# Two transposes of a transformer block moved from TensorE and ScalarE to transposing transfers, and VectorE's small tiles moved to PSUM

## The reference

```
# branch 1: linear attention, 16 heads of 16
qkv = x @ Wqkv.T + bqkv ;  q, k, v = split(qkv)
q = elu(q * scale) + 1 ;   k = elu(k * scale) + 1
y = q * cumsum(k * v) / clip(sum_d(q * cumsum(k)), 1e-3)
x = layernorm(x + y @ Wproj.T + bproj)
# branch 2: feed-forward in block floating point, blocks of 32 share a power of two
h = gelu(quant(x) @ quant(w_fc).T + b_fc)            # 256 -> 1024
x = layernorm(x + quant(h) @ quant(w_proj).T + b_proj)   # 1024 -> 256
```

## Time and profile before

| | |
|---|---|
| runs of the kernel before | 281.45, 281.32, 280.38 us; median 281.32 us |
| the profiled execution | 282.59 us |
| its span (first to last instruction) | 280.8 us |
| PE busy | 252.6 us, 90% |
| DVE busy | 243.3 us, 87% |
| ACT busy | 168.8 us, 60% |
| POOL busy | 169.9 us, 60% |
| mean granted TensorE clock | 0.976 of full speed |

### The profile page before, as it was taken

The page is one execution under the profiler, slowest core; times in us unless marked ns, Lnnn a source line. Parts: engine busy times, 40 slices in busy tenths (PEclk is TensorE's granted clock), DMA queues, the critical chain, the costliest instruction groups (busy, mean ns, idle before and its releaser), DMA issues.

```text
span 280.8 us, 4189 instructions
## 1 busy us (share of the span) xinstructions
PE 252.6 (90%) x1476; PEld 158.1 (56%) x1476; DVE 243.3 (87%) x505; ACT 168.8 (60%) x278; POOL 169.9 (60%) x113
## 2 busy tenths in 40 slices
PE   5798998999999999999999999999999998858650
PEld 4545553665575656675676557655766565633330
DVE  2289788989899989999899989998999999987941
ACT  0563426757669576848676856866694766345712
POOL 1056365666856594777568666759565947763831
PEclk9799799999999999999999999999999999999995
DMA  6930020002001300030002200220001000200202
GB/s 162 363 76 2 0 75 2 0 2 75 0 2 49 103 1 1 2 120 30 2 0 75 78 1 0 77 75 0 2 25 50 4 0 0 77 1 0 75 2 75
DMA packets 13556, 11.82 MB, mean 42 GB/s; under 512 B 3040, under 2 KB 13280, under 8 KB 13536
## 3 DMA queue, kind: packets, MB, share of 16 engines
q1 hardware_dynamic: 11904, 11.28, 12.5%
q10 hardware_dynamic: 1632, 0.27, 0.6%
HBM read 7.35 MB, written 4.19 MB: 41 GB/s over the span
## 4 chain that ended last, share of the span: by engine, by line
DVE 51%; PE 34%; POOL 4%; ACT 3%; issue 3%; DMA 3%; ACTq 1%; POOLq 0%; DVEq 0%
PE abank L964 19%; DVE h_amax L748 11%; DVE stats L722 7%; DVE kvsum L700 6%; DVE hq L659 5%; PE dbank L1028 4%; DVE y L712 3%; DVE r L716 3%; DMA Wproj_sb<-in_L_attn_Wproj_dram 3%; DVE h_pow L651 2%; PE tbank L1021 2%; PE bbank L996 2%; DVE kv L690 2%; DVE r L760 2%; PE hbank L1014 2%
## 5 line engine op out<-in xcount | busy, mean ns | idle before, releaser
L964 PE MATMUL abank<-xT,WqkvT 128*128 128x512 f32 x176 | 85.3, 609 | 0.8 <-ACT xT L429 0.8
L323 POOL TENSOR_TENSOR h_round<-h,h_inv 128x1024 f16<-128x1024 f32 x32 | 73.7, 2302 | 16.2 <-DVE h_inv L654 16.2
L964 PEld LDWEIGHTS abank<-xT,WqkvT 128*128 128x128 f32 x176 | 30.5, 192 | 24.3 <-issue 22.3
L444 ACT ACTIVATE h<-hbank 128x512 f32<-128x512 f32 x64 | 36.4, 593 | 9.6 <-PE hbank L1014 9.2
L438 ACT ACTIVATE expz<-abank,zbias_neg 128x512 f32<-128x512 f32 x30 | 20.6, 687 | 32.4 <-PE abank L964 32.1
L748 DVE TENSOR_REDUCE h_amax<-h 128x32 f32<-128x1024 f32 x32 | 38.7, 1209 | 1.2 <-ACT h L444 1.2
L1014 PE MATMUL hbank<-w_fcT,xqT 128*128 128x512 bf16 x128 | 38.1, 379 | 0.0
L308 POOL TENSOR_TENSOR rstd<-vareps,minus_half 128x4 f32<-128x4 f32 x16 | 18.4, 1151 | 32.4 <-DVE vareps L734 32.4
L1028 PE MATMUL dbank<-w_prT,hT 128*128 128x256 bf16 x256 | 33.3, 273 | 3.6 <-ACT hT L454 3.6
L299 POOL TENSOR_TENSOR qk<-qf,ksum 128x512 f32<-128x512 f32 x16 | 22.0, 1379 | 20.8 <-DVE qf L683 17.2
L303 POOL TENSOR_TENSOR num<-qf,kvsum 128x512 f32<-128x512 f32 x16 | 27.2, 1715 | 10.4 <-DVE kvsum L700 10.4
(11 more groups left out here) (100 smaller groups left out, 409.9 us busy)
## 6 DMA issues: line engine op xcount, KB each, us to landing
x_sb<-in_L_attn_x_dram SPq DMA_DIRECT2D x8, 512.0 KB, 3.6
out_dram<-o_sb SPq DMA_DIRECT2D x7, 512.0 KB, 2.9
h<-in_L_ffn_w_fc_dram SPq DMA_DIRECT2D x1, 1024.0 KB, 10.9
h<-in_L_ffn_w_proj_dram SPq DMA_DIRECT2D x1, 1024.0 KB, 12.6
Wqkv_sb<-in_L_attn_Wqkv_dram SPq DMA_DIRECT2D x1, 512.0 KB, 6.6
out_dram<-o_sb SPq DMA_DIRECT2D x4, 128.0 KB, 1.7
Wqkv_sb<-in_L_attn_Wqkv_dram SPq DMA_DIRECT2D x1, 256.0 KB, 7.7
Wproj_sb<-in_L_attn_Wproj_dram ACTq DMA_DIRECT2D x1, 256.0 KB, 7.9
```

The source lines that it names most:

```text
L323: nc.gpsimd.tensor_tensor(h_round[:, t % 2].rearrange("p (g j) -> p g j", j=BLOCK_K), h[:, t].rearrange("p (g j) -> p g j", j=BLOCK_K), h_ ...
L444: nc.scalar.activation(h[:, t, half * HALF:(half + 1) * HALF], hbank[half][:, :], ACT.Gelu).then_inc(s_h, 1)
L964: last = nc.tensor.matmul(ps[:, :], WqkvT[:, k, e * P:(e + 1) * P], xT[:, k], start=(k == 0), stop=(k == CC - 1))
```

## The change

Five things are changed together.

1. xq and hq are turned by transfers. `turn_xq` and `turn_hq` start one transposing transfer each from SP, 128x1024 in bf16 (256 KB), from xq to xqT and from hq to hT. PE's eight transposes and ACT's copy are gone, four times a chunk for hq and once for xq. xqT has another layout, which `up` reads accordingly. hT has three buffers in place of two (HT = 3), with a semaphore each, and `turn_hq` waits until `down` of three tiles earlier is done. `turn_xq` waits until all eight `up` of the chunk before are done.
2. tbank becomes vbank, a PSUM bank that only DVE uses: it holds a single column of ones, h_amax, x_amax, w_amax, stats and mv. The scans read the one with a step of zero in place of `ones_row`.
3. `mean_var` takes four bn_aggr and two small instructions in place of the six small ones.
4. The store does not wait for itself on SP any more: ACT's `norm_2` waits for the transfer's semaphore directly.
5. All engines have a new order. The loop has 4 steps, the other parts are written out.

The core of the diff:

```diff
+    HT = 3
-        ones_row = sb("ones_row", [P, TOK])
-        xqT = sb("xqT", [P, CC, TOK], BF16)
+        xqT = sb("xqT", [P, TILES, CC, P], BF16)
-        hT = sb("hT", [P, 2, HC, P], BF16)
+        hT = sb("hT", [P, HT, HC, P], BF16)
-        tbank = bank("tbank")
+        vbank = bank("vbank")
+        one = vbank[:, 0:1]
+        h_amax = vbank[:, 8:8 + TILES * HB].rearrange("p (t g) -> p t g", t=TILES)
+        x_amax = vbank[:, 136:136 + TILES * XB]
+        w_amax = vbank[:, 168:168 + 2 * HC * XB].rearrange("p (n g) -> p n g", n=2)
+        stats1, stats2 = (vbank[:, 296 + 24 * n:320 + 24 * n].rearrange("p (t s) -> p t s", t=TILES) for n in range(2))
+        mv1, mv2 = (vbank[:, 344 + 8 * n:352 + 8 * n].rearrange("p (t s) -> p t s", s=2) for n in range(2))
...
+            def turn_xq(n):
+                wait(sp, s_xq, n + 1)
+                wait(sp, s_h_ps, 8 * n)
+                sp.dma_start_transpose(xqT[:, :, :, :].rearrange("p t c n -> p (t c) n"),
+                                       xq[:, :, :].rearrange("p t c -> p (t c)")).then_inc(s_xqT, 16)
+            def turn_hq(n, t):
+                wait(sp, s_hq, 4 * n + t + 1)
+                wait(sp, s_down, 4 * n + t + 1 - HT)
+                slot = (4 * n + t) % HT
+                sp.dma_start_transpose(hT[:, slot], hq[:, t]).then_inc(s_hT[slot], 16)
...
-            def transpose_xq(n):
-                wait(pe, s_xq, n + 1)
-                for c in range(CC):
-                    for t in range(TILES):
-                        last = nc.tensor.transpose(t16[:, c * TOK + t * P:c * TOK + (t + 1) * P], xq[:, t, c * P:(c + 1) * P], ident16[:, :])
-                last.then_inc(s_xqT_ps, 1)
-            def copy_xqT(S):
-                wait(act, s_xqT_ps, S + 1)
-                nc.scalar.copy(xqT[:, :, :].rearrange("p c n -> p (c n)").bitcast(U32), tbank[:, :].bitcast(U32)).then_inc(s_xqT, 1)
...
-                nc.vector.tensor_tensor_scan(ksum[:, b, c], ones_row[:, :], kf[:, c], ksum[:, b, c, TOK - 1:TOK],
+                nc.vector.tensor_tensor_scan(ksum[:, b, c], one.broadcast_to([P, TOK]), kf[:, c], ksum[:, b, c, TOK - 1:TOK],
                                              ALU.mult, ALU.add).then_inc(s_ksum, 1)
...
-                nc.vector.tensor_tensor(mv[:, 0], mean_e, mean_o, ALU.add)
-                nc.vector.tensor_tensor(mv[:, 1], mean_e, mean_o, ALU.subtract)
-                nc.vector.scalar_tensor_tensor(mv[:, 2], m2_e, C * LN_EPS, m2_o, ALU.add, ALU.add).then_inc(s_mv, 1)
-                wait(dve, s_mv, 2 * S + 1)
-                nc.vector.tensor_scalar(negmean[:, :], mv[:, 0], -0.5, None, ALU.mult)
-                nc.vector.scalar_tensor_tensor(mv[:, 3], mv[:, 1], 0.25, mv[:, 1], ALU.mult, ALU.mult).then_inc(s_mv, 1)
-                wait(dve, s_mv, 2 * S + 2)
-                nc.vector.scalar_tensor_tensor(vareps[:, :], mv[:, 2], 1.0 / C, mv[:, 3], ALU.mult, ALU.add).then_inc(s_ve, 1)
+                for t in range(TILES):
+                    last = nc.vector.bn_aggr(mv[:, t], stats[:, t])
+                last.then_inc(s_mv, 1)
+                wait(dve, s_mv, S + 1)
+                nc.vector.tensor_scalar(negmean[:, :], mv[:, :, 0], -1.0, None, ALU.mult)
+                nc.vector.tensor_scalar(vareps[:, :], mv[:, :, 1], LN_EPS, None, ALU.add).then_inc(s_ve, 1)
```

More of the change, by code:

```diff
@@ new lines, in _, with step @@
+            turn_hq(0, 0)
+            turn_hq(0, 1)
+            load(3)
+            turn_hq(0, 2)
+            turn_hq(0, 3)
+            turn_xq(1)
+            def step(s):
+                n = s + 1
+                turn_hq(n, 0)
+                turn_hq(n, 1)
+                n = s
+                store(n)
+                n = s + 4
+                load(n)
+                n = s + 1
+                turn_hq(n, 2)
+                turn_hq(n, 3)
+                n = s + 2
+                turn_xq(n)
@@ new lines, in _ @@
+            for s in range(STEPS):
+                step(s)
+            turn_hq(5, 0)
+            turn_hq(5, 1)
+            store(4)
+            turn_hq(5, 2)
+            turn_hq(5, 3)
+            turn_xq(6)
+            turn_hq(6, 0)
+            turn_hq(6, 1)
+            store(5)
+            turn_hq(6, 2)
+            turn_hq(6, 3)
+            turn_xq(7)
+            turn_hq(7, 0)
+            turn_hq(7, 1)
+            turn_hq(7, 2)
+            turn_hq(7, 3)
+            store(6)
+            store_last(7)
@@ L826, in step @@
                 n = s
-                residual_2(n, n % 2, 1)
+                quantise_h(n, 3)
                 n = s + 2
@@ L868, in step @@
                 residual_1(n, n % 2, 1)
+                mean_var_1(n)
             for s in range(STEPS):
                 step(s)
+            h_exponents(4, 3)
+            quantise_h(4, 2)
+            residual_2(4, 0, 0)
+            feature(6, 1, 0, abank[0])
+            sum_k(6, 0, 0)
+            feature(6, 0, 0, abank[1])
+            quantise_h(4, 3)
+            multiply_kv(6, 0, abank[0])
+            x_exponents(5, 1)
+            residual_2(4, 0, 1)
+            sum_kv(6, 0, 0)
+            feature(6, 1, 1, abank[1])
+            quantise_x(5)
+            residual_2(4, 0, 2)
+            feature(6, 0, 1, abank[0])
+            sum_k(6, 0, 1)
+            multiply_kv(6, 1, abank[1])
+            residual_2(4, 0, 3)
+            mean_var_2(4)
+            denominator(6)
+            sum_kv(6, 0, 1)
+            h_exponents(5, 0)
+            attention_out(6, 0)
+            attention_out(6, 1)
+            h_exponents(5, 1)
+            quantise_h(5, 0)
+            residual_1(6, 0, 0)
+            h_exponents(5, 2)
+            quantise_h(5, 1)
+            residual_1(6, 0, 1)
+            mean_var_1(6)
             h_exponents(5, 3)
-            mean_var_1(6)
             quantise_h(5, 2)
```

470 lines of the change are left out of this document (228 added, 242 removed).

## The result

| | before | after |
|---|---|---|
| median of the runs | 281.38 us (280.38 to 283.59, 4 runs) | 286.70 us (285.62 to 287.42, 4 runs) |
| ratio, 95% interval | | 1.0175 (1.0106 to 1.0244) |
| the profiled execution | 282.59 us | 287.42 us |
| its span | 280.8 us | 285.6 us |
| mean granted TensorE clock | 0.976 | 0.943 |

The change makes the kernel slower, by 5.3 us between the medians and 4.8 between the profiled executions. The prediction said 3.1 us faster.

A forecast was written before the change was run, and what follows sets the result against it. DVE's own stream, 28.95 of a 29.88 us step, was taken as the bound once PE's transposes go; -4.7 middle, -1.0 beginning and +2.6 end sum to -3.1, from 281.32 to 278.2 us; range 275 to 293.

The forecast's parts named there:

- L: Latency of a turned transfer, from the end of DVE's xq or hq to data in SBUF: 3.0 us, before 1.35.
- Middle, -4.7: Loop steps: six, each 29.1 us against 29.88 by shorter DVE work and fewer waits, 6 x -0.78 = -4.7 us.
- Beginning, -1.0: Start of the kernel: cheaper first scan, later xq(0), one `up` fewer ahead of `denominators(1)`; -1.0 us, between 0 and -1.9.
- The scan's -1.8: Beginning: the first scan beside POOL's rounding of w_fc takes 1.28 us, not 3.05, saving 1.8 us on the chain.
- Taking w_exponents first sends the bias rows 6 us later, hidden: Beginning: the later bias rows cost nothing, as `project_out(0)` comes 10 us after.
- End, +2.6: Last chunk, a chain without cover: two longer transfer latencies, +3.3 us, less 0.7 for one h_pow, make +2.6 us.
- the "-0.7" for h_pow: End: one h_pow, read from PSUM, need not wait for POOL's rounding, 0.2 us instead of 0.87, saving 0.7.
- 2 x 1.65: End: xq(7) to `up` and the last tile's hq to `down` each take 1.65 us longer, +3.3 us.
- The break-even at L = 3.5: Whole kernel: at a turned-transfer latency of 3.5 us the change would neither gain nor lose.
- xq did not come late: Rival, chance 0.30: latency over 3.5 us holds `up`, so DVE waits every step; 288 us at 4.3, 295 at 5.1.
- The freed time was used: Rival, chance 0.10, claimed the opposite: steps stay near 29.9 us, +1.6 us, 283 us, between 281 and 284.
- PSUM is not dear: Rival, chance 0.06, claimed the opposite: 34 DVE instructions a step cost up to 53 ns more each, 1.8 us; 287 us.

The follow-up runs named there:

- e7: The changed kernel with plain transfers of the same bytes in place of the transposing ones: 286.12 us, 1.0147 to the kernel before.
- e11: The changed kernel run once more, unedited: 285.48 us, 1.0130 to the kernel before.
- e1: The changed kernel with the bias rows split before w_exponents(0), as before the change: 285.45 us, 1.0134 to the kernel before.
- e13: The changed kernel with only the last chunk's DVE pieces in an order as before: 284.05 us, 1.0064 to the kernel before.
- e9: The changed kernel with short idle matmuls fitted into PE's waits for hT of the last two chunks: 284.03 us, 1.0091 to the kernel before.
- e14: The changed kernel with bias rows split first, short idle matmuls in PE's late waits, and the last chunk's DVE order as before: 280.53 us, 0.9919.
- e6: The changed kernel with a second transposing transfer of xq, which nobody reads, ahead of each one that counts: 307.81 us, 1.0911 to the kernel before.

## Why the prediction was wrong

The sign was wrong. The result lies inside the stated range only because of the rivals that widened it, and for none of their reasons.

**L, right.** 3.0 taken, 3.0 landing; from the end of xq(7) to `up` 3.1. It came from sound steps: a plain transfer of the size was put at 2.1 us and takes 2.3 (e7), and turning was put at 0.9 more and adds 0.7. On the way to it the prediction set aside the Trainium skill's 1309 ns a block (VectorE: DVE Perf Modes, The three transpose paths): eight blocks at that price are 10.5 us, and the trace disagrees. Another page fits: DMA: Bandwidth & Descriptors, Latency and other measured facts, gives 261 GB/s for transposing transfers with a non-contiguous middle dimension, 1.0 us for 256 KB; with the 2 us of fixed cost that SBUF — State Buffer, The DMA setup-cost knee, states, an estimate from the two pages is 3.0, and the trace agrees.

**Middle, -4.7, was -3.0.** The mechanism of the step was right, its size nearly: 29.26 for 29.1, which makes 0.8 of the missing 1.7 us over five steps. The step that failed is "Six steps: 6 x -0.78". Five are full ones and gave 3.15 us ((227.96 - 78.30) - (226.05 - 79.53)). The sixth, from xq(6) to xq(7), is 26.5 us after and 26.3 before, gaining nothing, the other 0.9: DVE's own work does not bound it, since it waits for x_round on POOL, 1.79 us after and 1.46 before.

**Beginning, -1.0, was +1.2 in one execution, -1.2 in another, and +0.5 on like clocks.** (The terms that the prediction lists give -0.8; nothing there makes it -1.0.) The scan's -1.8 came true. What failed is "Taking w_exponents first sends the bias rows 6 us later, hidden": it costed the transfers and not the DVE instruction, which met POOL's rounding for 3.47 us. The move costs 1.9 us at vareps(0) (e11 against e1). Without it the beginning would have brought some 1.5 us, an estimate from these two differences.

**End, +2.6, was +6.7.** By the rows: xq(7) to `up` 3.11 for 1.35, +1.75, as forecast. `up` to the end of the last hq 15.01 for 14.37, +0.65: the "-0.7" for h_pow did not come, because the wait for POOL moved one instruction on, to h_inv (0.60 at 263.34). The last hq to the last `down` 5.02 for 1.35, +3.65 where +1.65 stood. The last `down` to the end of r +0.65, the clock. So the two latencies of "2 x 1.65" were there, 1.75 each, and the transfers did not queue. The steps that failed are two: the -0.7, and the path. The prediction lets the last `down` wait for hT of the last tile alone; in the run it stands behind the three downs before it, which began late, behind hT of the first tile and PE's 5.47 us of idling, and ran at the lower clock. That path has 1.9 us of the 3.65 and the 0.65 behind it, for which the prediction had no term. The runs agree: the order gives back 1.4 us (e13), the fill that keeps the clock up 1.5 to 1.9 (e9, with its late transfer in it), both together 2.3 (e14 against e11). The 4.1 us that then remain are 3.5 of latency and 0.9 of the slow transfer beside the q8 packet, less 0.4 between.

**The break-even at L = 3.5** was wrong with the terms: e7 has L = 2.3 and is still slower than the kernel before (1.0147).

**The rivals.** xq did not come late; e6 shows that this rival's mechanism and its price a step were real, from 3.37 us on (forecast 3.3). Its evidence for a long L was not: the bias rows, 5.1 us before, land in 2.0 in the change, where the first leaves at 20.01 and not at 11.29, behind the loads of the weights. The freed time was used. PSUM is not dear: of the instructions in the loop x_pow, which no POOL work touches, shows the most, 194 to 224 ns, and the reductions 5 ns of 1209. The rival's 53 ns a piece is not borne out. Nor, in the loop, are the 65 ns by the Trainium skill's page (Perfetto Trace Analysis, Optimizing Scalar/DVE Operations); only w_pow, which reads 128x128 and runs twice in all, shows as much, 226 to 291. No rival named the mechanism that decided: a chain at the end whose first transfer comes late and which slows PE by making it wait.
